# A two-layer graph network on one core: when the slots of gathered rows are handed back in its two edge stages

## The reference

```python
# layer 0: graph attention, 4 heads of 64
h = (x @ W).reshape(N, 4, 64)
e = leaky_relu(a_src[src] + a_dst[dst], 0.2)
alpha = softmax of e over the edges of one destination
out = segment_sum(h[src] * alpha[:, :, None], dst)

# layer 1: tensor-product messages
w = silu(edge_scalars @ fc_w1 / sqrt(8)) * 1.679 @ fc_w2 / 8     # four weights of 64 per edge
xg = y[edge_src]                                                  # 256 features of the source node
mids = products of w, xg and edge_attr                            # 8 blocks of 64 per edge
agg = segment_sum(mids, edge_dst)
```

## Time and profile before

| | |
|---|---|
| median of 3 runs | 4414.33 us |
| the profiled execution | 4411.13 us |
| its span | 4409.4 us |
| PE busy | 3355.8 us (76%) |
| DVE busy | 2254.6 us (51%) |
| POOL busy | 1828.4 us (41%) |
| ACT busy | 1458.5 us (33%) |
| mean granted TensorE clock | 0.829 |
| gathers (L581, L1971) from `ix` | 805 and 804 |

### The profile page before, as it was taken

How to read it: one execution, slowest core, us unless ns; L and a number is a source line. 1 busy time by engine, 2 the same in 40 slices (tenths; PEclk the granted TensorE clock), 3 DMA queues, 4 the chain that set the end, 5 groups by cost and what they waited for, 6 DMA issues and landing times. The chain is left out here.

```text
span 4409.4 us, 78133 instructions
## 1 busy us (share of the span) xinstructions
PE 3355.8 (76%) x22728; PEld 2460.8 (56%) x22728; DVE 2254.6 (51%) x6165; ACT 1458.5 (33%) x4662; POOL 1828.4 (41%) x1962
## 2 busy tenths in 40 slices
PE   6576677767776678799867877778778877778679
PEld 4455566655665566688734444444444444446668
DVE  5445555555555467566634444444444444456732
ACT  5122222222222136233223333333333334323612
POOL 3555555555555421011154444444444444442134
PEclk9678777777777889899878777877788777888889
DMA  6333222333233346322232222222222222233611
GB/s 193 108 81 81 80 78 80 80 82 83 77 85 80 82 127 191 107 85 81 76 90 71 65 65 67 68 65 67 69 65 65 68 67 65 69 80 100 176 40 49
DMA packets 330288, 375.91 MB, mean 85 GB/s; under 512 B 179374, under 2 KB 236790, under 8 KB 329946
## 3 DMA queue, kind: packets, MB, share of 16 engines
q0 software_dynamic: 89712, 230.26, 18.8%
q1 hardware_dynamic: 238666, 140.84, 12.4%
q10 hardware_dynamic: 1696, 2.62, 0.2%
HBM read 310.75 MB, written 62.84 MB: 85 GB/s over the span
## 5 line engine op out<-in xcount | busy, mean ns | idle before, releaser
L1971 POOL DMA_INDIRECT e_rows<-tab,e_ix x804 | 762.0, 948 | 993.8 <-ACT e_ix L2016 789.5
L581 POOL DMA_INDIRECT e_rows<-tab,e_ix x805 | 763.1, 948 | 667.4 <-ACT e_ix L689 438.5
L982 PE MATMUL e_pU<-e_ohp,e_rows 128*128 128x128 f32 x3340 | 561.6, 328 | 154.9 <-issue 149.2
L2221 PE MATMUL e_pU<-e_msg,e_oh 128*32 128x128 f32 (+1 forms) x6672 | 507.2, 332 | 201.8 <-issue 197.2
L982 PEld LDWEIGHTS e_pU<-e_ohp,e_rows 128*128 128x128 f32 x3340 | 523.3, 241 | 186.6 <-issue 181.0
L2151 DVE TENSOR_TENSOR e_msg<-e_pW,e_rows 128x256 f32<-128x256 f32 x417 | 176.5, 423 | 869.8 <-remote 607.7
L2221 PEld LDWEIGHTS e_pU<-e_msg,e_oh 128*32 128x32 f32 x6672 | 281.5, 118 | 408.5 <-issue 351.0
L2153 DVE TENSOR_TENSOR e_msg<-e_pW,e_rows 128x384 f32<-128x384 f32 x834 | 422.2, 548 | 0.0
L2207 PE MATMUL e_pW<-e_w,e_hT 64*128 64x256 f32 x1668 | 374.9, 490 | 54.9 <-DVE e_msg L2153 26.1
L695 ACT CAST e_ohT<-e_pT 64x640 bf16<-64x640 f32 x167 | 114.7, 687 | 901.2 <-remote 504.7
L963 PE MATMUL e_pT<-ident,e_oh 128*64 128x128 f32 x835 | 152.2, 314 | 230.2 <-issue 117.2
(11 more groups left out here) (453 smaller groups left out, 5988.8 us busy)
## 6 DMA issues: line engine op xcount, KB each, us to landing
e_rows<-tab,e_ix POOLq DMA_INDIRECT x1609
xnT<-f_xnT SPq DMA_DIRECT2D x25, 250.0 KB, 3.0
e_xk<-xnT SPq DMA_DIRECT2D x25, 250.0 KB
xnT<-b_xT SPq DMA_DIRECT2D x25, 250.0 KB, 3.0
m_xnT<-xnT SPq DMA_DIRECT2D x25, 250.0 KB
xnT<-m_xT SPq DMA_DIRECT2D x25, 250.0 KB, 2.7
ffn_norm<-xnT SPq DMA_DIRECT2D x25, 250.0 KB
tab<-f_hrow SPq DMA_DIRECT2D x25, 227.5 KB
```

The source lines that it names most:

```text
L581: nc.gpsimd.indirect_dma_start(out=rows[:, s, j, :], out_offset=None, in_=env["tab0"], in_offset=bass.IndirectOffsetOnAxis(ap=at[:, j:j + ...
L982: nc.tensor.matmul(pU[:, s % 2, 2 * W * k:2 * W * (k + 1)], rows[:, s, j, 128 * k:128 * k + 128], ohp[:, s % 3, j, 2 * k:2 * k + 2, :], st ...
L1971: nc.gpsimd.indirect_dma_start(out=rows[:, r % PER, j, :], out_offset=None, in_=env["tab1"], in_offset=bass.IndirectOffsetOnAxis(ap=at[:, ...
L2221: last = nc.tensor.matmul(u8[:, 0:8:2, :] if c == 0 else u8[:, 1:2 + 2 * c:2 * c, :], oh[:, r % 2, ST * i + j, c, :], m[:, 0:4, :] if c == ...
```

## The change

In the first edge stage PE's second product of each tile at L982 now raises a new semaphore, `s_rel` (five per group). ACT copies the indices of a group as soon as the first tile of the group that had its slot before is summed, and POOL waits before each tile's gather until the same tile of that former group is summed. In the second stage ACT waits only for the first pair of messages of the former group, and POOL waits ahead of each pair of gathers for the same pair of messages.

```diff
-        s_eq = sem("e0_equal")
+        s_eq, s_rel = sem("e0_equal"), sem("e0_tile_summed")
 ...
                         for j in range(GT):
+                            if lo >= SLOTS:
+                                hold(pool, s_rel, GT * (g - SLOTS) + j + 1)
                             nc.gpsimd.indirect_dma_start(
 ...
                         if lo >= SLOTS:
-                            hold(act, s_acc, g - SLOTS + 1)
+                            hold(act, s_rel, GT * (g - SLOTS) + 1)
                             nc.scalar.copy(ix[:, s, :], srcI[:, bass.ds(g * GT, GT)]).then_inc(s_ix, 1)
 ...
                             for k in range(2):
-                                nc.tensor.matmul(...)
+                                last = nc.tensor.matmul(...)
+                            last.then_inc(s_rel, 1)
 ...
-                        for j in range(T1):
-                            nc.gpsimd.indirect_dma_start(
-                                ...).then_inc(s_gat[r % PER], 16)
+                        for i in range(PAIRS):
+                            if lo >= PER:
+                                hold(pool, s_msg, PAIRS * (g - PER) + i + 1)
+                            for j in (2 * i, 2 * i + 1):
+                                nc.gpsimd.indirect_dma_start(
+                                    ...).then_inc(s_gat[r % PER], 16)
 ...
                         if lo >= PER:
-                            hold(act, s_msg, PAIRS * (g - PER + 1))
+                            hold(act, s_msg, PAIRS * (g - PER) + 1)
```

More of the change, by code:

```diff
@@ L981, in sums @@
                             for k in range(2):
-                                nc.tensor.matmul(pU[:, s % 2, 2 * W * k:2 * W * (k + 1)], rows[:, s, j, 128 * k:128 * k + 128],
-                                                 ohp[:, s % 3, j, 2 * k:2 * k + 2, :], start=j + k == 0, stop=j == GT - 1,
-                                                 skip_group_check=True)
+                                last = nc.tensor.matmul(pU[:, s % 2, 2 * W * k:2 * W * (k + 1)],
+                                                        rows[:, s, j, 128 * k:128 * k + 128],
+                                                        ohp[:, s % 3, j, 2 * k:2 * k + 2, :], start=j + k == 0,
+                                                        stop=j == GT - 1, skip_group_check=True)
+                            last.then_inc(s_rel, 1)
                         for j in range(GT):
@@ L1112, in edges0 @@
         window_loop(env, iota, one_pass, s_gat,
-                    s_dw + [s_ix, s_oh, s_eq, s_T, s_ohT, s_E, s_lg, s_ed, s_p, s_ohp, s_acc, s_add,
+                    s_dw + [s_ix, s_rel, s_oh, s_eq, s_T, s_ohT, s_E, s_lg, s_ed, s_p, s_ohp, s_acc, s_add,
                             s_xk, s_kv, s_sq, s_ss, s_sd, s_kvn, s_ks, s_qw, s_wq, s_bp, s_kvb, s_pb,
@@ L1969, in step @@
                             hold(pool, s_ix, g - PER + 1)
-                        for j in range(T1):
-                            nc.gpsimd.indirect_dma_start(
-                                out=rows[:, r % PER, j, :], out_offset=None, in_=env["tab1"],
-                                in_offset=bass.IndirectOffsetOnAxis(ap=at[:, j:j + 1], axis=0))\
-                              .then_inc(s_gat[r % PER], 16)
+                        for i in range(PAIRS):
[3 more added lines that the diff above has]
+                                nc.gpsimd.indirect_dma_start(
+                                    out=rows[:, r % PER, j, :], out_offset=None, in_=env["tab1"],
+                                    in_offset=bass.IndirectOffsetOnAxis(ap=at[:, j:j + 1], axis=0))\
+                                  .then_inc(s_gat[r % PER], 16)
                     turns(pool, step)
```

## The result

The changed kernel takes 4470.07 us (median of 4 runs, 4461.51 to 4470.71), beside 4416.9 us for the kernel before in runs on the same chip. The ratio is 1.0116, with a 95% interval of 1.0104 to 1.0129: about 52 us slower. The forecast was 4416 us, with a range up to 4436 us. It was wrong: the measured time lies 34 us above the top of the range.

A forecast was written before the change was run, and what follows sets the result against it. Waits bound the kernel: DVE's stops at runs of gathers, with no engine full. Nothing saved, 2 us lost to later starts: 4411.1 to 4413 us profiled, the median 3.2 us above, so 4416 us; range 4400 to 4436.

The forecast's parts named there:

- No reader waits for a gather, and a run of gathers holds the others until it has drained: Both edge stages: gathered rows lie ready some 14 us, POOL's 1228 us are slack; DVE stops until a run ends.
- The release on ACT: ACT's index copies, both stages: the old waits never held, so 0 us saved, at most 4.1; added register instruction 0.05 us.
- The waits on POOL: Ahead of gathers, 805 and 402 waits: all met, hidden behind the gather ahead, 0.01 us or less each, off everybody's path.
- The increments on PE: PE's first-stage products: 835 more increments cost 0, upper bound 0.05 us each, 42 us in all.
- The first gather of a group starts 0.1 us later, and a tenth of it reaches the end: POOL's runs in both stages: 236 starts 0.1 us later, 24 us if all reached the end, 2 us taken.
- The first rival: DVE's 65 + 132 stops each move out 0.1 us with their run: 20 us slower, 4434 us; chance 14%.
- The second: Waits ahead of POOL's gathers cost 0.47 us each, lengthening runs: 114 us slower, 4528 us; chance 5%.
- The runs fall apart: First stage: waits or later starts part two groups' gathers, 4 of 65 stops of 7.2 us go: 4385 us; chance 12%.
- The change does what it says: Indices and gathers come earlier but rows only lie longer before their readers: the same 4414 us; chance 3%.
- the slack of 14 us: First stage: a group's gathered rows lie in their slot some 14 us before its exponents are taken.
- The prediction's own sign of being wrong: DVE's remote waits changing by over 9 us in sum, or index copies or gathers moving by over a few tenths.
- Its sign that POOL would have no wait for PE's products or DVE's messages: POOL in the profile after: no wait for PE's products at L982 or DVE's messages, a sign of being right.

The follow-up runs named there:

- the pieces alone: Kernel before plus six met waits ahead of ACT's second-stage loop, nothing changed in the loop: 4488.83 us, ratio 1.003 (1.0016 to 1.0044).
- with the release: Kernel before plus PE's increments and ACT's two new waits ahead of the index copies, POOL as before: 4441.04 us, ratio 1.0046.
- the inner waits: Kernel before plus PE's increments and POOL's waits only ahead of tiles 2 to 5 (first stage), pairs 2 and 3 (second): 4448.99 us, ratio 1.0072.

## Why the prediction was wrong, step by step

- **No reader waits for a gather, and a run of gathers holds the others until it has drained: right** on the chip of the forecast. It is also where the slip lies: having named the stop as what binds, the working priced each edit by what it does to its own engine, and not by what it does to the stop.
- **The release on ACT, cost 0: wrong.** The waits were indeed met, and nothing was saved or lost by them. But ACT's program grew by register instructions, priced at 0.05 us each where they stand, and this moved the loop's head. That gave 2.4 us of idle time on average in each of ten passes, and cost 13 to 20 us of the 52 (1.003 for the pieces alone, 1.0046 with the release). The row was there to be compared, and the prediction even named the 4.1 us as the most that could be gained; it didn't ask what could be lost in that place.
- **The waits on POOL, hidden behind the gathers, cost 0: wrong in the sum, right on POOL.** The pace is 1.25 us with them, on either kind of chip. Whatever one read takes, even eight fit into the 1.25 us from one gather to the next. Yet in the stages that stop, the inner waits cost 32 us (19 to 44), and waits on a constant that was met all along cost 11 and 22 us. The step that failed is "off everybody's path": between the gathers of a run they were not, though POOL itself never lost time by them.
- **The increments on PE, cost 0: right** (0.9999).
- **The first gather of a group starts 0.1 us later, and a tenth of it reaches the end: the start is right, 0.13 us, and its cost is none** (0.9992). The 2 us of the sum were not there.
- **The first rival**, each stop moving out with its run, gave the sign and the place that would show it (DVE's remote waits, +41 and +61 us), but not the cause: the later start alone is free. Why DVE's long pieces have grown is open. **The second**, dear waits ahead of gathers, was nearest in what it blamed, but its mark, 1.7 us between gathers, did not come. **The runs fall apart:** by the traces some did, 45 runs of ten gathers instead of 51 (49 with the increments alone, 47 with the inner waits), but its mark, fewer long pieces at DVE's logits, did not come (69 against 65), and the stage got longer. With one trace each these counts may be scatter. **The change does what it says:** nothing was gained by an earlier release, as the slack of 14 us said.

The range rested on terms that were all bounded by rows of POOL and ACT, and none was for a stop that changes with the instruction stream. Measured, that term is 32 us, 3% of DVE's 1020 us of remote waits. Nothing in the rows of before gave its size. The prediction's own sign of being wrong, a change of DVE's remote waits by over 9 us in sum, came with 102 us. Its sign that POOL would have no wait for PE's products or DVE's messages failed by name only (222.4 and 97.8 us), since these waits were met.

## What to carry to other kernels

Price an edit twice: on its own engine, and on whatever really binds. A wait that never holds is free where it stands and can still cost at a distance, by moving a loop's head in the program, or by standing in a run of gathers while another engine is being held (by what path is open); look at the first work behind a loop's branch before and after. And before a loss of one per cent is put down to the code, run it on a second chip: this one is 1.0116 on a chip that takes 4417 us and 0.999 on one that takes 3329.

## What the runs showed of the hardware that was not expected

- The same kernel takes 4417 and 4477 us on two chips and 3329 and 3327 us on two others, with gathers of 946 to 949 ns each (medians) on all. For the changed kernel nearly all of the difference lies in the two edge stages: 1444 and 1774 us against 1010 and 1104.
- On the slower two, late in a run of ten indirect gathers in the first stage, TensorE starts one product every 1.4 to 2.8 us until the run has drained; on the faster chip whose trace is shown TensorE keeps its 2.40 us for twenty, with gathers running.
- ACT's loop over ten groups can lose 2.4 to 2.8 us at each branch back by where its head lies: six instructions more ahead of it brought the idle time in the kernel before, eight more took it away in the changed one.
- A wait that is met between two gathers of GpSimd leaves them 1.25 us apart, and even so 644 such waits made the program 11 us (4 to 18) longer on a chip with the stops.
